# Rotary tables renewed by half sequence, norms gathered to 128x32 with a Newton step on GpSimd, and a new order of all engines

## What is computed

```python
x = L0_attn_x                                   # (4, 512, 128), float32
x = x + attention(_layernorm(x), Wq, Wk, Wv, Wr)      # 16 heads of 64, causal
x = x + _L0_ffn_ref(_layernorm(x), ...)
# _L0_ffn_ref, DEPTH = 6, HEADS = 16, DIM_HEAD = 64, WINDOW = 32:
for i in range(DEPTH):
    x = attn_layer(shift_tokens(x), Wqkv[i], q_scale[i], k_scale[i], Wo[i]) + x
    x = ffn_layer(shift_tokens(x), ln_g[i], ln_b[i], W1[i], b1[i], W2[i], b2[i]) + x
# attn_layer: q, k = l2norm(q) * q_scale, l2norm(k) * k_scale; rotary with a scale by position;
#   softmax over the own window of 32 and the one before it; times v; @ Wo
# ffn_layer: layer norm; hg = xn @ W1 + b1; a * gelu(gate) @ W2 + b2
# shift_tokens: the upper half of the channels comes from the token before
```

## Time and profile before

| | us |
|---|---|
| median of 3 runs (lowest, highest) | 2483.86 (2482.43, 2490.55) |
| profiled execution | 2478.85 |
| its span in the profile | 2477.0 |
| PE, DVE, ACT, POOL busy | 2240.8, 1696.9, 1281.8, 1463.3 |
| mean granted clock of TensorE | 0.952 |

### The profile page before, as it was taken

The page is one execution under the profiler, slowest core; times in us unless marked ns, Lnnn a source line. Parts: engine busy times, 40 slices in busy tenths (PEclk is TensorE's granted clock), DMA queues, the critical chain, the costliest instruction groups (busy, mean ns, idle before and its releaser), DMA issues. The chain is left out here.

```text
span 2477.0 us, 60119 instructions
## 1 busy us (share of the span) xinstructions
PE 2240.8 (90%) x23184; PEld 1255.8 (51%) x23184; DVE 1696.9 (69%) x3412; ACT 1281.8 (52%) x2402; POOL 1463.3 (59%) x1342
## 2 busy tenths in 40 slices
PE   8999999976889899998999989999899998999985
PEld 4545455533445455554555545555455554555542
DVE  5556555546767678776787767877668776787752
ACT  5565565632454455544555445554455544565442
POOL 3344433336666677666776667766666676676740
PEclk9999999987999999999999999999999999999997
DMA  1000000023343533445334353344534435344330
GB/s 56 6 1 5 1 5 1 1 65 96 90 114 99 145 89 97 114 100 143 88 96 114 101 143 89 96 113 102 143 88 105 112 93 143 95 101 110 93 86 21
DMA packets 219577, 208.27 MB, mean 84 GB/s; under 512 B 44194, under 2 KB 211104, under 8 KB 217760
## 3 DMA queue, kind: packets, MB, share of 16 engines
q1 hardware_dynamic: 219296, 204.45, 32.4%
HBM read 83.79 MB, written 13.63 MB: 39 GB/s over the span
## 5 line engine op out<-in xcount | busy, mean ns | idle before, releaser
L722 POOL TENSOR_TENSOR T<-T,RB 128x512 f32<-128x512 f32 x384 | 487.1, 1300 | 264.7 <-DMA RB<-norms 264.7
L647 PE MATMUL bank<-XT,WQK 128*128 128x256 f32 x1536 | 460.4, 426 | 155.6 <-DVE T L668 131.7
L673 POOL TENSOR_TENSOR T<-T 128x512 f32<-128x512 f32 x384 | 503.4, 1317 | 127.5 <-DVE T L668 127.4
L756 PE MATMUL bank<-WU,XT 128*32 128x512 f32 x3072 | 431.7, 635 | 1.7 <-ACT U L763 1.6
L647 PEld LDWEIGHTS bank<-XT,WQK 128*128 128x128 f32 x1536 | 278.1, 201 | 250.6 <-DVE T L668 151.7
L653 ACT ACTIVATE SQ<-bank 128x512 f32<-128x512 f32 x384 | 227.7, 593 | 296.0 <-PE bank L647 295.3
L413 POOL TENSOR_SCALAR PR<-PR,RI 128x512 f32<-128x512 f32 x256 | 173.9, 692 | 314.4 <-DVE RI L354 314.4
L763 ACT ACTIVATE U<-bank 128x512 f32<-128x512 f32 x384 | 229.3, 597 | 178.7 <-PE bank L853 140.3
L667 DVE TENSOR_TENSOR T<-bank,TAB 128x512 f32<-128x512 f32 x384 | 260.9, 679 | 83.0 <-ACT SQ L653 47.7
L349 DVE CUSTOM_DVE_ANT_0 PR<-bank,causal 128x512 f32<-128x512 f32 x256 | 174.3, 682 | 201.4 <-PE bank L192 201.3
L818 POOL TENSOR_TENSOR PL<-PL,RIL 128x512 f32<-128x512 f32 x192 | 201.3, 1048 | 143.9 <-DVE RIL L811 143.9
(11 more groups left out here) (110 smaller groups left out, 3463.3 us busy)
## 6 DMA issues: line engine op xcount, KB each, us to landing
RB<-norms SPq DMA_DIRECT2D x384, 128.0 KB, 3.1
KZ<-T SPq DMA_DIRECT2D x384, 128.0 KB, 2.6
QP<-T SPq DMA_DIRECT2D x192, 256.0 KB, 4.3
TAB<-rotary_dram SPq DMA_DIRECT2D x12, 1024.0 KB, 8.2
norms<-RN SPq DMA_DIRECT2D x96, 128.0 KB, 2.5
WQK<-wqk_halves_dram SPq DMA_DIRECT2D x12, 512.0 KB, 6.0
WVS<-wv_turned_dram SPq DMA_DIRECT2D x30, 128.0 KB, 2.5
WOS<-wo_lanes_dram SPq DMA_DIRECT2D x30, 128.0 KB, 2.7
```

Source lines behind the costliest of these rows:

```text
L647: m = pe.matmul(b[:, ab * HALF:(ab + 1) * HALF], WQK[:, kind, i, ab, :], XT[s % 2][:, hf * HALF:(hf + 1) * HALF], start=True, stop=True)
L673: pool.tensor_tensor(t1, t1, T2[i % 2][:, ::-1, :], ALU.add).then_inc(l_rotated.sem, 1)
L722: pool.tensor_tensor(t1, t1, RB[:, i:i + 1, :].to_broadcast([P, 2, HALF]), ALU.mult).then_inc(l_scaled.sem, 1)
L756: i = pe.matmul(bank[1][h * WIN:(h + 1) * WIN, :], XT[s % 2][:, c0:c0 + WIN], WU[:, lp * HG + h, :], start=True, stop=True)
```

## The change

1. The tables are loaded and scaled in four parts per layer (kind and half of the sequence) instead of two, each up to three slots ahead of its use; `WQK` has three buffers of one kind instead of two, and its load has a place of its own.
2. `dve_clamp` writes `SS` (128x256, of which four rows in 32 carry sums). `sp_gather_sums` moves these by four DMAs into `SM`, 128x32. Ln and Exp run on 128x32, and the Newton step is four GpSimd instructions on 128x32 (`pool_newton`) instead of three of DVE on 128x256. The write of the norms to DRAM is 128x32. `sp_norms` is split into `sp_norms_out` and `sp_norms_in`.
3. The feed-forward's norm: DVE keeps the statistics; `veps`, the negated mean, the power and their product are four POOL instructions; the scaling is four ACT instructions instead of four of DVE. `pool_ffn_b2` adds the second bias to `X` after the product down has been added, and the next turn of that `X` waits for it.
4. All five lists are in a new order.

```diff
-            WQK = sbl('WQK', [P, 2, HG, 2, P])
+            WQK = [sbl(f'WQK{i}', [P, HG, 2, P]) for i in range(3)]
...
+            def sp_load_table(l, part):
+                hf, kind = divmod(part, 2)
+                cols = slice(hf * HALF, (hf + 1) * HALF)
                 if l:
-                    sp.wait_ge(l_front_done.sem, l_front_done.at(last))
-                    sp.wait_ge(l_products.sem, l_products.at(last))
-                sp.dma_start(WQK[:, kind, :, :, :], wqk[l, :, kind, :, :, :]).then_inc(s_wk[kind], 16)
-                sp.dma_start(TAB[:, kind, :, :, :], rot[kind]).then_inc(s_wk[kind], 16)
+                    sp.wait_ge(l_products.sem, l_products.at((l - 1) * 16 + 12 + part))
+                sp.dma_start(TAB[:, kind, :, :, cols], rot[kind, :, :, :, cols]).then_inc(s_tb[part], 16)
...
             def dve_clamp(f):
                 dve.wait_ge(l_sums_done.sem, l_sums_done.at(f))
-                dve.wait_ge(l_newton.sem, l_newton.at(f - 1))
-                dve.wait_ge(l_guess.sem, l_guess.at(f - 1))
-                dve.tensor_scalar(SM[:, :], bank[4][:, 0:HALF], FAR, NORM2_EPS, ALU.min, ALU.max).then_inc(l_clamped.sem, 1)
+                dve.wait_ge(s_sc, 64 * f)
+                dve.tensor_scalar(SS[:, :], bank[4][:, 0:HALF], FAR, NORM2_EPS, ALU.min, ALU.max).then_inc(l_clamped.sem, 1)
+
+            def sp_gather_sums(f):
+                sp.wait_ge(l_clamped.sem, l_clamped.at(f))
+                sp.wait_ge(l_newton.sem, l_newton.at(f - 1))
+                for j in range(HG):
+                    r = slice(j * WIN, (j + 1) * WIN)
+                    sp.dma_start(SM[r, :], SS[j * WIN:j * WIN + HG, :].rearrange('h (t c) -> h t c', c=WIN)).then_inc(s_sc, 16)
...
+            def pool_newton(f):
+                pool.wait_ge(l_guess.sem, l_guess.at(f))
+                pool.tensor_tensor(Y2[:, :], Y0[:, :], Y0[:, :], ALU.mult).then_inc(l_newton.sem, 1)
+                pool.wait_ge(l_newton.sem, l_newton.at(f, 0))
+                pool.tensor_tensor(Y2[:, :], Y2[:, :], SM[:, :], ALU.mult).then_inc(l_newton.sem, 1)
+                pool.wait_ge(l_newton.sem, l_newton.at(f, 1))
+                pool.tensor_scalar(Y2[:, :], Y2[:, :], -0.5, 1.5, ALU.mult, ALU.add).then_inc(l_newton.sem, 1)
+                pool.wait_ge(l_newton.sem, l_newton.at(f, 2))
+                pool.wait_ge(s_rn, 16 * f)
+                pool.tensor_tensor(RN[:, :], Y0[:, :], Y2[:, :], ALU.mult).then_inc(l_newton.sem, 1)
...
             def sp_slot(k):
+                if hold_f(k + 3):
+                    sp_relayout(k + 3)
+                if step_at(k + 3, LAST + 1, 1):
+                    sp_next_vo((k + 3) // 4)
+                if hold_f(k + 4):
+                    sp_norms_in(k + 4)
+                if hold_f(k + 5):
+                    sp_gather_sums(k + 5)
...
+                if change_at(k + 9, 4):
+                    sp_load_table(*divmod(k + 9, 16))
+                if change_at(k + 7, 2):
+                    sp_load_weights(*divmod(k + 7, 16))
                 if hold_f(k + 5):
-                    sp_norms(k + 5)
...
+                    sp_norms_out(k + 5)
+                if step_at(k - 2, LAST - 1):
+                    sp_shift((k - 2) // 4)
```

More of the change, by code:

```diff
@@ L710, in sp_norms, with sp_norms_in @@
                 sp.dma_start(norms[f % 2], RN[:, :]).then_inc(s_rn, 16)
+            def sp_norms_in(f):
                 sp.wait_ge(s_rn, 16 * (f + 1))
                 sp.wait_ge(l_scaled.sem, l_scaled.at(f - 1))
[L713 removed]
+                rows = norms[f % 2].rearrange('(g h t a) c -> h a g (t c)', h=HG, t=8, a=1)
                 for h in range(HG):
@@ L1002, in half_at, with step_at, change_at @@
                 return v % 2 == 0 and 0 <= v // 2 < 2 * STEPS
-            def step_at(v, last):
-                return v % TPB == 0 and 0 <= v // TPB <= last
-            def change_at(v):
-                return v % 16 < 2 and 0 < v // 16 < DEPTH
+            def step_at(v, last, first=0):
+                return v % TPB == 0 and first <= v // TPB <= last
+            def change_at(v, n):
+                return v % 16 < n and 0 < v // 16 < DEPTH
             def layer_at(v):
@@ L1059, in pe_slot @@
                 if here(k + 2):
+                    pe_scores(*tile(k + 2), 0)
+                if step_at(k + 1, LAST):
+                    pe_next_vo((k + 1) // 4)
+                if here(k + 2):
+                    pe_scores(*tile(k + 2), 1)
                     pe_u(*tile(k + 2), 0)
+                if step_at(k - 5, LAST - 1):
+                    pe_ffn_up((k - 5) // 4, 3)
                 if here(k + 1):
                     pe_values(*tile(k + 1), 0)
+                    pe_values(*tile(k + 1), 1)
@@ L1091, in act_slot @@
+                    dve_shift(*tile(k + 2), 1)
+                    dve_sums(*tile(k + 2), 0)
                 if hold_f(k + 6):
-                    act_square(k + 6, 2)
+                    dve_products(k + 6, 1)
                 if here(k + 2):
-                    act_keep_u(*tile(k + 2), 2)
+                    dve_sums(*tile(k + 2), 1)
+                if 0 < k + 6 < BATCH:
+                    dve_ln2(k + 6)
+                if here(k + 1):
+                    dve_residual(*tile(k + 1))
@@ new lines, in pool_slot @@
+                if 0 < k + 4 < BATCH:
+                    pool_ln2(k + 4)
+                if hold_f(k + 2):
+                    pool_scale(k + 2, 3)
+                if here(k):
+                    pool_normalise(*tile(k), 0)
+                if hold_f(k + 4):
+                    pool_rotate(k + 4, 0)
+                if here(k):
+                    pool_normalise(*tile(k), 1)
+                if hold_f(k + 4):
+                    pool_rotate(k + 4, 1)
+                    pool_rotate(k + 4, 2)
@@ L1213, in pe_layers_program @@
             def pe_layers_program():
-                for k in range(-7, TOTAL + 2):
+                for k in range(-7, TOTAL + 1):
                     pe_slot(k)
@@ L1238, in dve_layers_program @@
                 dve_ln2(0)
-                for k in range(-7, TOTAL + 3):
+                for k in range(-7, TOTAL + 2):
                     if k == 0:
@@ L1252, in pool_layers_program @@
                 pool.wait_ge(s_i, 16 * NI)
-                for kind in range(2):
-                    pool_fold_scale(0, kind)
-                for k in range(-7, TOTAL + 2):
+                for part in range(4):
+                    pool_fold_scale(0, part)
+                for k in range(-7, TOTAL + 1):
                     pool_slot(k)
+                pool_ffn_b2(LAST - 1)
                 pool_ffn_norm(LAST)
@@ L1261, in sp_layers_program @@
                 sp.dma_start(QSC[:, :], qsc).then_inc(s_i, 16)
-                for kind in range(2):
-                    sp_load_front(0, kind)
+                sp_load_weights(0, 0)
+                sp_load_table(0, 0)
+                sp_load_weights(0, 1)
+                for part in range(1, 4):
+                    sp_load_table(0, part)
                 sp_next_vo(0)
@@ L1268, in sp_layers_program @@
                 sp.dma_start(B2A[:, :, :], b2.rearrange('(a l) e -> a l e', a=1).to_broadcast([P, DEPTH, E])).then_inc(s_i, 16)
-                for k in range(-7, TOTAL + 2):
+                for k in range(-7, TOTAL + 1):
                     sp_slot(k)
                 sp_shift(LAST)
-                for kind in range(2):
-                    sp.wait_ge(s_wk[kind], 32 * DEPTH)
+                for i in range(3):
+                    sp.wait_ge(s_wk[i], 16 * (2 * DEPTH // 3))
+                for part in range(4):
+                    sp.wait_ge(s_tb[part], 16 * DEPTH)
+                sp.wait_ge(s_sc, 64 * FRONTS)
                 sp.wait_ge(s_i, 16 * NI)
```

307 lines of the change are left out of this document (136 added, 171 removed).

## The result

The changed kernel takes 2513.8 us (median of four runs, 2510.2 to 2517.4) against 2484.2 in the runs beside it: a ratio of the means of 1.0114, 95% interval 1.0091 to 1.0138. The time lies within the whole range of the prediction (2400 to 2550) but outside the forecast's own (2425 to 2500), and the direction is the other one: 30 us more by the medians where I had 22 less.

What follows compares the result with a forecast made beforehand. A POOL and SP ring bounded the old step (75.3 us); PE's path (76.2 with scatter) would set the new. Span 2477 + 20 - 30 - 8 - 3 = 2456, median 2462 us, range 2400 to 2550.

Steps and rivals of the forecast that it cites:

- the right ring: POOL's scaling and SP's relayout, norm write and read wait for each other in turn; about 75.3 us a step before.
- The ring alone: Two K and two Q turns, 4 x (10.1 + 4.96 + 1.1), plus 1.5 + 1.3 + 7.3 for the shift: 74.7 us a step.
- The rival that the read lands late: Relayout and read take 11.5 us instead of 10.1, deciding from 10.5; ring 80.3, time 2552; 26%.
- PE's path: From residual through shift, relayout, read and scalings to PE's turn of probabilities: 67.3 + 6.2 stall + 2.5 half clock = 76.0.
- slot B: PE's slot after the one ending the step's last tile: 14.2 us plus halves down, merged weights and turn, 18.6.
- The rival of broken waits: PE waits in three places (U copy, turn, probabilities), 2 us each; clock never falls; step 73.6, time 2405; 15%.
- The shift: Between norm write and next K relayout, 8.0 us of issue with nothing covering it; 7.3 in the ring sum.
- Newton step on POOL: Four 128x32 instructions ahead of the last scaling, 0.22 us each plus waits: 1.1 us a front; DVE's relief gives nothing.
- The gather: Four small DMAs between clamp and guess, 3.4 us with issue, up to 6 behind other packets; nothing in the ring.
- The rival of small packets: Gather's 128-byte rows make it take 6 us or more; PE's chain needs 11 us against 10.3; time 2480; 9%.
- Change of layer: Table parts issued three slots ahead; extra per layer-change step falls from 7 us to 1: 5 x (7 - 1) = -30.
- Ends: First six fronts without a shift -8 us; last tiles with less feed-forward work, less the bias, -3 (+3 to -6).

Runs made afterwards that it cites:

- the experiment on it: Changed kernel with the two loads of the next weights issued behind the read and the gather instead of between relayout and read: 2478.9 us, 0.9973 of before.
- the guess experiment: Changed kernel with ScalarE's guess of the norms made behind the slot's first exponential and first U copy instead of ahead: 2519.8 us, 1.0148 of before.
- the cut: Second shift DMA cut into 126 partitions and 1: 2399.9 us (0.9658) in the changed kernel, 2437.9 (0.9831) in the kernel before.
- the early read: The kernel with the four edits, plus norms read into two RB buffers ahead of shift and relayout, query-key weights in two buffers: 2357.9 us, 0.95.
- The undoing: Changed kernel with both table halves of a kind loaded together behind the layer's last products of that kind, folded one slot later: 2617.3 us, 1.0539.
- the same kind of move, for the norm and for the Newton step: Norm behind fourth scaling, on the kernel with the four edits: 2425.3 us. Newton step on VectorE: 2427.8 there, 2614.9 on the changed kernel.
- the kernel with the four edits: Changed kernel with shift DMA cut 126+1, next weights behind the gather, guess behind the U copy, second bias behind the fourth scaling: 2338.9 us, 0.9417.

## Why the prediction was wrong

It had the right ring and the right terms, but took the wrong one of its two sums for the larger.

- **The ring alone, 74.7.** This is the step that failed. Measured in the step shown it is 78.3: 42.85 instead of 40.4 from relayout to scaling, four times 6.15 instead of 6.06 for scalings and Newton step, 1.9 instead of 1.5 for the norm, 1.25 (1.3) for the bias, 7.6 instead of 7.3 for the shift. Of the 3.6 us that it was short, 2.4 are the reads. Two turns are near the 10.1 taken; the third has the next weights between relayout and read (+1.5), which the sum left out, though `sp_next_vo` stands there in the diff; the experiment on it gave 35 us. The first, behind the shift, is 0.7 longer; why is open.
- **The rival that the read lands late** is in substance what happened: a mean of 10.7 to 10.8, where it said that it decides from 10.5. By its own formula with the means of all turns, 4 x (10.77 + 4.96 + 1.22) + 1.9 + 1.3 + 7.6 = 78.6. It had 26%. Its price, 2552, was too high, since it took 11.5 for the read. The reason given for it misread the rows: 4.8 and 5.0 us are no scatter of over 1 us.
- **PE's path, 76.0.** No single stall of 6.2 us came; the longest in a plain step is 4.0. PE stands in five places and more, mostly 0.9 to 3 us each, about 9.2 us a step, because it follows the ring; the guess experiment showed that these waits have no price of their own. (In this sum, too, the parts of the feed-forward add up to 11.1 and not 10.4; that changes slot B by 0.1.) The rival of broken waits had the places right, but not that the clock stays up, nor the time.
- **The shift.** Its price was seen and its size right (8.0 of issue, 7.6 bare). It was called the price of the change, and it is: the cut gave 114 us here and 47 in the kernel before.
- **Newton step on POOL.** 0.24, 0.25, 0.22 and 0.25 us, 1.22 with waits against 1.1. Right. That DVE's relief gives nothing no run tests alone.
- **The gather.** Issue 2.8, and from its first issue to the guess 4.1 us on the mean of each slot (3.4 taken); the guess was hardly ever what POOL waited for in this kernel (4.0 us in all 96 fronts). It is not in the ring here; with the early read POOL waits for the guess 351.4 us in all. The rival of small packets needed 6 us or more for it, and did not come about. (The prediction says that the trace of before has no DMA with rows under 512 bytes; the shift's own rows of 256 are under it.)
- **Change of layer.** 5 x 1 said; the five are no longer than the others. Right as to what the new profile shows. The undoing shows that the halves are needed, not the size of 30.
- **Ends.** -8 and -3 said. The first shift comes 13.0 us earlier (675.3 against 688.3), and from the last shift to the end it is 1.2 us more (47.7 against 46.5): the sum is near, and that is luck in part, since the end went the other way.

Put together: 52 us are missing between 2456 and 2508.4. The plain step grew by 3.7 us (74.9 to 78.6), not by 0.9, x22 = 61 of them: 2.4 of the 2.8 a step because the ring is the longer, at 78.6 and not 76.2, and 0.4 because the 74.9 holds the last step before, 68.9 long; the other sixteen have a mean of 75.3, as was taken. The layer change gave 39 back, 5 x (7.5 + 0.4), where 30 were said.

## What to carry to other kernels

Where an engine's list and a DMA queue wait for each other in turn, sum every instruction that stands in that circle, loads for others too, turn by turn and not with one mean; if the result is within some per cent of the busiest engine's path, do not trust which is larger. What left this circle left the step at its full price (5, 1.6 and 1.3 us), until other chains were level with it, and waits of the busiest engine may be mere followers of it. But something moved out may be what the next chain waits for: the same kind of move, for the norm and for the Newton step, cost 86 to 101 us.

## What the runs showed of the hardware

- A DMA of 127 partitions to 127 (rows of 256 bytes) blocks the next issue on its queue for 6.4 us; cut into 126 and 1 it does not. The block follows the DMA and not the one that is issued late. While it moves, the 16 DMA engines are busy to 0.08 and move 18 GB/s, against 0.65 and 144 with 126 partitions.
- VectorE needs 1.07 us for a product on 128x32 with both inputs in SBUF while GpSimd works (0.19 in the two cases where it rested), GpSimd 0.25 for the same. Small steps of that kind can be cheaper on the engine that is called slow.
- The issue of the read took 3.4 us behind a Q relayout and 2.0 behind a K relayout, for the same four DMAs (medians); what was issued just before them is what differs.
- In nearly all steps of the changed kernel, where PE waits 2.4 to 4.0 us once and mostly 1 to 3 us again soon after, the mean granted clock is 0.96: for 6.8 us of most of them it is at the level of 1.2 GHz. In most steps of the cut shift, where the waits are under 2 us, the clock is 1.000, the 2.4 GHz level throughout. But in the kernel with two read buffers steps with one wait of 2.4 to 3.1 us kept 1.000, and in the kernel with the four edits a step whose longest wait was 1.9 us did not: the longest wait alone does not tell them apart.
